# Causal attention between two spiking FFNs: another layout of the diagonal maximum units, scores first in a slot, and the loads of the next heads in two steps

## The reference

```python
scores = jnp.einsum('bhsd,bhtd->bhst', q, k) * scale
causal = jnp.triu(jnp.ones((S, S), dtype=bool), k=1)
scores = jnp.where(causal, -jnp.inf, scores)
probs = jax.nn.softmax(scores, axis=-1)
out = jnp.einsum('bhst,bhtd->bhsd', probs, v)
```

## Time and profile before

| | us |
|---|---|
| three runs | 1600.67, 1615.71, 1618.32 |
| median | 1615.71 |
| the profiled execution | 1608.4 |
| its span, first to last instruction | 1606.7 |
| PE busy | 1381.6 (86%) |
| DVE busy | 1139.5 (71%) |
| ACT busy | 860.6 (54%) |
| mean granted clock of PE | 0.904 of full speed |

### The profile page before, as it was taken

How to read it: one execution, slowest core, us unless ns; L and a number is a source line. 1 busy time by engine, 2 the same in 40 slices (tenths; PEclk the granted TensorE clock), 3 DMA queues, 4 the chain that set the end, 5 groups by cost and what they waited for, 6 DMA issues and landing times. The chain is left out here.

```text
span 1606.7 us, 27137 instructions
## 1 busy us (share of the span) xinstructions
PE 1381.6 (86%) x8384; PEld 821.8 (51%) x8384; DVE 1139.5 (71%) x2689; ACT 860.6 (54%) x1155; POOL 229.9 (14%) x206
## 2 busy tenths in 40 slices
PE   5988888750799999999999989999999976899997
PEld 5877777640443343343343333433433422799986
DVE  5666676821788888877887887888888930567675
ACT  5644444310036666655665665666666655466564
POOL 0012222346001011010010110110110101110100
PEclk9999999875568899997997999999999978899999
DMA  5113333437152062070080260440620002222312
GB/s 204 40 40 105 105 118 100 150 123 95 13 69 34 6 83 24 5 101 8 9 98 5 30 82 5 55 52 6 72 34 5 8 8 68 92 80 92 95 51 66
DMA packets 101898, 97.86 MB, mean 61 GB/s; under 512 B 46288, under 2 KB 85200, under 8 KB 100048
## 3 DMA queue, kind: packets, MB, share of 16 engines
q1 hardware_dynamic: 101744, 95.98, 29.0%
HBM read 57.15 MB, written 37.75 MB: 59 GB/s over the span
## 5 line engine op out<-in xcount | busy, mean ns | idle before, releaser
L1001 ACT ACTIVATE probs<-s_ps 128x1024 f32<-128x1024 f32 (+3 forms) x640 | 542.7, 895 | 327.7 <-PE s_ps L1133 326.4
L1112 PE MATMUL m_ps<-kT,qT 64*128 64x512 f32 (+3 forms) x1280 | 478.9, 478 | 112.9 <-DMA qT<-qkT_parts 55.9
L1026 DVE TENSOR_REDUCE maxes<-m_ps 128x1 f32<-128x512 f32 x768 | 490.8, 684 | 48.5 <-PE m_ps L1112 44.2
L1112 PEld LDWEIGHTS m_ps<-kT,qT 64*128 64x128 f32 x1280 | 217.2, 201 | 502.2 <-DVE maxes L1026 274.0
L1133 PE MATMUL s_ps<-qT,kT 64*128 64x512 f32 (+3 forms) x1280 | 327.3, 416 | 13.8 <-DMA qT<-shiftT 10.5
L1031 DVE CUSTOM_DVE_ANT_0 masked<-m_ps,mask_b 128x384 f32<-128x384 f32 (+3 forms) x512 | 238.3, 488 | 130.6 <-PE m_ps L1112 125.0
L1150 PE MATMUL o_ps<-probs,v_w 128*32 128x512 f32 (+3 forms) x2560 | 322.4, 578 | 0.2 <-POOL probs L974 0.2
L974 POOL TENSOR_SCALAR_AFFINE_SELECT probs<-probs 128x512 f32<-128x512 f32 x128 | 81.6, 637 | 851.8 <-ACT probs L1001 851.8
L1133 PEld LDWEIGHTS s_ps<-qT,kT 64*128 64x128 f32 x1280 | 164.2, 198 | 41.0 <-ACT probs L1001 25.0
L313 ACT ACTIVATE relu_a<-ups_a 128x512 f32<-128x512 f32 x64 | 38.1, 596 | 100.8 <-PE ups_a L562 99.9
L1150 PEld LDWEIGHTS o_ps<-probs,v_w 128*32 128x32 f32 x2560 | 51.9, 111 | 76.5 <-issue 58.9
(11 more groups left out here) (124 smaller groups left out, 1917.7 us busy)
## 6 DMA issues: line engine op xcount, KB each, us to landing
kT<-qkT_parts SPq DMA_DIRECT2D x48, 256.0 KB
qT<-qkT_parts SPq DMA_DIRECT2D x96, 128.0 KB
qkT_parts<-qk_hi_a SPq DMA_DIRECT2D x32, 256.0 KB, 3.0
qkT_parts<-qk_lo_a SPq DMA_DIRECT2D x32, 256.0 KB, 3.4
qT<-shiftT SPq DMA_DIRECT2D x512, 1.0 KB
xin_a<-in_x SPq DMA_DIRECT2D x8, 512.0 KB, 4.0
xres_a<-in_x SPq DMA_DIRECT2D x8, 512.0 KB, 4.9
x<-xsum_a SPq DMA_DIRECT2D x8, 512.0 KB, 3.2
```

What stands on the lines that cost most here:

```text
L1001: act.activation(probs[:, b % PBUF, 2 * hp:2 * hp + 2, off:CH], s_ps[hp][:, :, off:CH], ACT.Exp, scale=D ** -0.5)\
L1026: dve.tensor_reduce(out, m_ps[:, bank, 0:width], AX.X, ALU.max).then_inc(max_read, 1)
L1112: pe.matmul(m_ps[:, bank, 0:width], qT[of % 2][r0:r0 + HR, j, h // 2, t * P:(t + 1) * P], kT[of % 2][r0:r0 + HR, h // 2, k * CH:k * CH + w ...
```

## The change

Four edits, all in `attention_phase`. A diagonal square of a head and a step becomes three units in the place of four: TRI holds the four triangles of 128 keys side by side, over a mask that an identity matmul in bf16 writes into the bank first; WIDE and NARROW hold the rectangles between them, 512 and 256 columns. DVE reduces each with one `tensor_reduce` over several tiles. A group has 144 units. In a slot PE issues both head pairs' scores first and then the units. SP issues terms 0 and 1 of the next group's load at j = 0, and term 2 at j = 1. SP no longer waits for DVE before it loads the mask. The diff without empty lines:

```diff
-        mask = sb("mask_b", [P, CH])
-        masked = sb("masked", [P, 2, CH])
-        maxes = sb("maxes", [P, 2, G, T, NJ])
+        mask = sb("mask_b", [P, P])
+        masks, identb = sb("masks", [P, T, P], BF16), sb("identb", [P, P], BF16)
+        maxes = sb("maxes", [P, 2, G, T, FULL + NJ - 1])
...
-        UNITS = [(j, t, 2 * hp + par, k, CH if k < j else P * (t + 1))
-                 for j in range(NJ) for t in range(T) for hp in range(G // 2) for k in range(j + 1) for par in range(2)]
+        def diagonal(j, h):
+            k0 = j * CH
+            return [(j, h, [(t, t * P, k0 + t * P, P) for t in range(T)], CH, slice(0, T), TRI),
+                    (j, h, [(2, 0, k0, 2 * P), (3, 2 * P, k0, 2 * P)], CH, slice(2, 4), WIDE),
+                    (j, h, [(1, 0, k0, P), (3, P, k0 + 2 * P, P)], 2 * P, slice(1, 4, 2), NARROW)]
+        UNITS = []
+        for j in range(NJ):
+            UNITS += [(j, 2 * hp + par, [(t, 0, k * CH, CH)], CH, slice(t, t + 1), FULL + k)
+                      for t in range(T) for hp in range(G // 2) for k in range(j) for par in range(2)]
+            UNITS += [diagonal(j, 2 * hp + par)[part] for hp in range(G // 2) for part in range(3) for par in range(2)]
...
-            sp.wait_ge(mask_ok, 1)
-            sp.dma_start(mask[:, CH - P:CH], w["mask"]).then_inc(const_in, 16)
+            sp.dma_start(mask[:, :], w["mask"]).then_inc(const_in, 16)
...
-                if j < 3 and exists(i, dn + 1):
+                if j < 2 and exists(i, dn + 1):
...
-                    load(i, dn + 1, (j,))
+                    load(i, dn + 1, ((0, 1), (2,))[j])
...
-            dve.memset(mask[:, :], 0.0).then_inc(mask_ok, 1)
+            dve.memset(maxes[:, :, :, :, :], NEG).then_inc(neg_fill, 1)
             dve.wait_ge(const_in, 32)
+            dve.tensor_copy(masks[:, :, :], mask[:, :].unsqueeze(1).broadcast_to([P, T, P])).then_inc(mask_ok, 1)
+            dve.tensor_copy(identb[:, :], ident[:, :]).then_inc(mask_ok, 1)
...
-                out = maxes[:, j % 2, 2 * (h % 2) + h // 2, t, k:k + 1]
-                if k < j:
-                    dve.tensor_reduce(out, m_ps[:, bank, 0:width], AX.X, ALU.max).then_inc(max_read, 1)
-                else:
-                    dve.wait_ge(max_read, done - 1)
-                    dve.sem_inc(passed_max, 1)
-                    dve.tensor_tensor_reduce(masked[:, u % 2, 0:width], m_ps[:, bank, 0:width], mask[:, CH - width:CH], 1.0, NEG,
-                                             ALU.add, ALU.max, out).then_inc(max_read, 1)
+                out = maxes[:, j % 2, 2 * (h % 2) + h // 2, tiles, column]
+                dve.tensor_reduce(out, m_ps[:, bank, 0:width].rearrange("p (n c) -> p n c", n=out.shape[1]), AX.X, ALU.max)\
+                   .then_inc(max_read, 1)
...
+                if column == TRI:
+                    pe.matmul(m_ps[:, bank, :], identb[:, :], masks[:, :, :].rearrange("p t k -> p (t k)"), start=True, stop=True)
                 r0 = HR * (h % 2)
-                pe.matmul(m_ps[:, bank, 0:width], qT[of % 2][r0:r0 + HR, j, h // 2, t * P:(t + 1) * P],
-                          kT[of % 2][r0:r0 + HR, h // 2, k * CH:k * CH + width], start=True, stop=True)\
-                  .then_inc(max_done, 1)
+                for t, c0, k0, keys in pieces:
+                    mm = pe.matmul(m_ps[:, bank, c0:c0 + keys], qT[of % 2][r0:r0 + HR, j, h // 2, t * P:(t + 1) * P],
+                                   kT[of % 2][r0:r0 + HR, h // 2, k0:k0 + keys], start=(column != TRI), stop=True,
+                                   skip_group_check=True)
+                mm.then_inc(max_done, 1)
...
+                    scores(i, dn, j, b, 0)
+                    scores(i, dn, j, b, 1)
                     some(0)
-                    scores(i, dn, j, b, 0)
                     some(1)
-                    scores(i, dn, j, b, 1)
                     some(2)
...
-            pe.wait_ge(const_in, 32)
+            pe.wait_ge(mask_ok, 2)

```

More of the change, by code:

```diff
@@ L696, in attention_phase @@
         HR, MB = P // 2, 3
+        TRI, WIDE, NARROW, FULL = 0, 1, 2, 3
         qT = [sb(f"qT{p}", [P, NJ, G // 2, CH], F32R) for p in range(2)]
@@ L726, in attention_phase @@
         mask_ok, bias_in = sem("mask_ok"), sem("bias_in")
-        passed, passed_max = sem("passed_b"), sem("passed_max")
+        passed, neg_fill = sem("passed_b"), sem("neg_fill")
         o_read, denom_done, att_out = (sem(n) for n in ("o_read", "denom_done", "att_out"))
@@ L743, in attention_phase @@
         SLOTS = NJ * (NJ + 1) * T // 2
-        UNITS = [(j, t, 2 * hp + par, k, CH if k < j else P * (t + 1))
-                 for j in range(NJ) for t in range(T) for hp in range(G // 2) for k in range(j + 1) for par in range(2)]
+        def diagonal(j, h):
[8 more added lines that the diff above has]
+            UNITS += [diagonal(j, 2 * hp + par)[part] for hp in range(G // 2) for part in range(3) for par in range(2)]
         MAX_FROM, MAX_TO = -20, 20
         def place_units():
-            cost = [u[4] + 110 for u in UNITS]
+            cost = [u[3] + 110 for u in UNITS]
             room = []
@@ L1015, in _ @@
                 dve.memset(kT[0][HR * par + HR // 2:HR * (par + 1), :, :].bitcast(F32), 1.0).then_inc(ones_ok[0], 1)
-            dve.memset(mask[:, :], 0.0).then_inc(mask_ok, 1)
+            dve.memset(maxes[:, :, :, :, :], NEG).then_inc(neg_fill, 1)
             dve.wait_ge(const_in, 32)
+            dve.tensor_copy(masks[:, :, :], mask[:, :].unsqueeze(1).broadcast_to([P, T, P])).then_inc(mask_ok, 1)
+            dve.tensor_copy(identb[:, :], ident[:, :]).then_inc(mask_ok, 1)
+            dve.wait_ge(neg_fill, 1)
             def unit(i, dn, x, ahead, u):
-                j, t, h, k, width = UNITS[u]
+                j, h, _, width, tiles, column = UNITS[u]
                 done, bank, _ = ring(i, dn, x, (ahead, u))
                 dve.wait_ge(max_done, done + 1)
-                out = maxes[:, j % 2, 2 * (h % 2) + h // 2, t, k:k + 1]
-                if k < j:
-                    dve.tensor_reduce(out, m_ps[:, bank, 0:width], AX.X, ALU.max).then_inc(max_read, 1)
-                else:
-                    dve.wait_ge(max_read, done - 1)
-                    dve.sem_inc(passed_max, 1)
-                    dve.tensor_tensor_reduce(masked[:, u % 2, 0:width], m_ps[:, bank, 0:width], mask[:, CH - width:CH], 1.0, NEG,
-                                             ALU.add, ALU.max, out).then_inc(max_read, 1)
+                out = maxes[:, j % 2, 2 * (h % 2) + h // 2, tiles, column]
+                dve.tensor_reduce(out, m_ps[:, bank, 0:width].rearrange("p (n c) -> p n c", n=out.shape[1]), AX.X, ALU.max)\
+                   .then_inc(max_read, 1)
                 return done + 1
@@ L1040, in negate @@
                     dve.wait_ge(max_read, found)
-                    dve.tensor_reduce(negmax[:, :], maxes[:, j % 2, :, :, 0:j + 1].rearrange("p h t k -> p (h t) k"), AX.X,
+                    dve.tensor_reduce(negmax[:, :], maxes[:, j % 2, :, :, 0:FULL + j].rearrange("p h t k -> p (h t) k"), AX.X,
                                       ALU.max, negate=True).then_inc(neg_step, 1)
@@ L1105, in find @@
                 of = dn + ahead
-                j, t, h, k, width = UNITS[u]
+                j, h, pieces, _, _, column = UNITS[u]
                 if u == 0:
```

## The result

The changed kernel takes 1653.99 us (median of 4 runs, 1647.56 to 1656.59), beside 1611.97 for the kernel before on the same chip (4 runs, 1600.67 to 1618.32). The ratio is 1.0263, 95% interval 1.0193 to 1.0332: slower by 2.6%. The forecast was 1639. The two profiled executions have spans of 1654.2 and 1606.7 us, 47.5 apart.

The account below looks back on a forecast made before the run. It took a closed PE-DVE loop (2.71 us per four-unit slot) as the bound, with shifts and loads as separate limits. 1608.4 + 25 + 2.4 + 17.6 - 5.6 - 2 - 1.4 - 5 gave 1639; range 1602 to 1662.

Parts of the forecast that it names:

- slots 0 to 11, groups 1 to 6 (loads): Two-step load delays slot 12 through the shifts of j = 2: +5.0 in four groups, +2.4 in two, +25 us.
- slots 12 to 19: Masked units in slots 17 to 19, less savings from fewer units: +2.2 us a group, +17.6 in eight groups.
- slots 20 to 23: Four masked units hidden behind SP's shift queue: no added time, PE's 11.6 us staying under 13.9.
- slots 24 to 39, with the clock: Fewer units against masked units, -5.6 us in seven groups, and a third of the possible clock gain, -5.
- lead-in: Before the first exponential: 72 units for 87, less DVE work but eight masked units at low clock, -2 us.
- start: SP starts the first load without waiting for DVE's memset: -1.4 us.
- the new units' +1.2: Net cost in slots 0 to 11 a group, hidden by slot 12's wait in groups 1 to 6.
- The masked unit: A TRI holds PE 1.0 us: 0.35 to the first triangle, 0.13 between triangles; bounds 0.43 and 1.3.
- Scores first: Issuing both head pairs' scores first in a slot: loop unchanged, taken as 0; 0.1 us a slot without one reduce.
- Loads hidden: Rival: shifts overtake the load or DMA runs faster, so the +25 goes; centre 1616 us, chance 0.26.
- Faster, with triangles beside the other half's work: Rival: a TRI costs PE only 0.43 us and the loads are hidden; 1587 us, chance 0.14.
- Slower on PE with 1.3 us a masked unit: Rival: each triangle takes 0.23 us and PE's clock falls in TRI slots; 1667 us, chance 0.12.

Follow-up runs that it names:

- e2: The kernel before with only the two-step load added: 1655.35 us, ratio 1.0293.
- e1: The changed kernel with the old loads, one term at the start of each step: 1620.02 us, ratio 1.0091.
- e5: The changed kernel with two att tiles and load term 2 issued in slot 6, behind the shifts of j = 2: 1628.7 us, ratio 1.0166.
- e3: The changed kernel with two att tiles and a semaphore for each: 1652.93 us, ratio 1.0288.
- e7: The kernel of e1 without the identity matmul, so the maximum is computed unmasked: 1590.37 us, ratio 0.9906.
- e6: The changed kernel with the old loads and the old order in a slot, the new diagonal layout alone: 1621.18 us, ratio 1.0130.
- e4: The changed kernel with the old order in a slot, units between the two head pairs' scores: 1648.7 us, ratio 1.0243.
- e8: The kernel before with only the new order in a slot, both head pairs' scores first: 1616.14 us, ratio 1.0067.
- e10: The kernel of e1 with eight shift DMAs of two rows in place of sixteen of one: 1586.42 us, ratio 0.9859.
- e9: The kernel before with eight shift DMAs of two rows in place of sixteen of one: 1602.15 us, ratio 0.9995.
- e11: The kernel of e1 with the masked units of a head pair issued together: 1608.35 us, ratio 1.0008.
- e12: The kernel of e11 with eight shift DMAs of two rows: 1573.58 us, ratio 0.9782.

## Why the prediction was right in sign and too low

By its own steps, in us, from the two profiled executions:

| step | forecast | measured |
|---|---|---|
| slots 0 to 11, groups 1 to 6 (loads) | +25 | +42.0 |
| slots 0 to 11, groups 0 and 7 | +2.4 | +2.2 |
| slots 12 to 19 | +17.6 | +15.4 |
| slots 20 to 23 | 0 | 0.0 |
| slots 24 to 39, with the clock | -10.6 | -11.2 |
| lead-in | -2 | +2.0 |
| start | -1.4 | -2.1 |
| after the last exponential | 0 | -0.9 |
| sum, before rounding | +31.0 | +47.5 |

**The step that failed is the size of the loads' term**, +17.0 in a sum that is short by 16.5. Its mechanism was right: e2 shows it alone, e1 shows it gone, e5 shows that the queue's order is what matters. Two things in it were wrong.

First, groups 2 and 4. The prediction laid the new wait over the 2.62 us of the back edge and took 2.4 a group. They measure +7.4 and +4.7 (and +7 each in 4 to 11 in e2). The price had been worked out at slot 12 only. The store of slot 3 holds DVE already in slot 7, as the upper bound of the step had it, and from there the slots up to 11 are late; in group 2 the back edge comes after it and is paid again (2.04 us). In group 4 PE's stall there is 2.23 us and ends with the shifts. e3 shows the overlap that the prediction had reckoned with: without the store's wait the edge lies under the wait for the shifts, and the two groups measure +4.4 and +4.3. So some 3 us of group 2 are the store's, and the rest is what the second point says. The prediction had the store going out at 587 and landing at 596 to 598, and still priced slot 12 alone.

Second, the +5.0 in the other four groups measures +6.9 to +8.1. ACT begins slot 12 37.4 us after the load's begin, forecast 35.9. The load's packets are through early (about 604, forecast 606.1). The shifts' small packets run among the last of them, those of the store issued at 602.56 behind them; the DMA line above shows work until slice 36, that is 606 to 607 us, and PE's scores start at 608.03. The forecast end was 1.5 us too early for slot 12, though too late for the load's own data; what held the shifts' landing between 604 and 608 isn't shown. That what lies ahead of slot 12 is hidden by this end, as the prediction had it for the new units' +1.2, is borne out by e3.

**The masked unit** was forecast at 1.0 us of PE, 0.35 from the identity to the first triangle and 0.13 between triangles. Measured in slot 17 of group 1: 0.91 us; 0.32 to the first triangle, then steps of 0.164, 0.112 and 0.109, and 0.20 until the array can take the products. The forecast from the transposes gave 0.39 for three steps, the runs 0.385. The rule of the Trainium skill, "TensorE: Matmul & The Clock Gate", section "Packing small matmuls", lets a weight load overlap running matmuls only where the row group differs, which with the page's figure for a load was an estimate of 0.16 a step; the trace agrees for the first step and not for the other two.

**Slots 12 to 19** came to +15.4 for +17.6, and that it came so near is partly luck. Slots 17 to 19 were forecast at +2.9 a group and measure +1.6 (slot 17 +1.0 for +1.5, slots 18 and 19 +0.3 each for +0.7); e7 shows that the identity matmul is the whole of it. The -0.7 that was to come off isn't there: slot 13 is 0.5 to 0.8 shorter, but slot 14 is 0.4 to 0.7 longer (groups 1 and 3). The rest, +2.3, is in groups 1 and 4, where the clock in slots 12 to 16 was 0.88 and 0.83 for 1.00 and 0.91.

In **slots 0 to 3** the size was right (+2.3 to +2.5 a group from group 1 on, forecast +2.6) and the cause only in part. The identity matmul is 1.0 to 1.3 of it (e7, groups at the full clock). The order in a slot, which the prediction took as 0, is 1.5 of it: with the old order and the identity matmul the new units cost 0.9 to 1.0 a group there (e6, and e4 alike). The two shares overlap, so they aren't to be added. The old layout shows no such cost of the order (e8, slots 0 to 3 as before). **Slots 20 to 23** stayed at 14.0 to 14.3, behind SP's queue, as forecast. e10 shows what was under that cover: 10.7, where the prediction's terms had 11.6.

**The lead-in** has the wrong sign. Fifteen units fewer were to outweigh eight masked ones at the low clock. e7 gives the missing price: without the identity matmuls the lead-in is 6.2 us shorter, 0.8 for each of its eight units, where 0.35 at the high clock was the row to hand.

**Scores first** was taken as 0. In the changed kernel that holds for the sum (e4), though not for its parts: e1 against e6, in groups 1 to 6, has +1.5 us a group in slots 0 to 3, about +0.9 in 20 to 23 and in 28 to 30, -0.7 in 17 to 19 and -1.6 in 31 to 39. Alone it costs 0.7% (e8), most of it in slots 24 to 30, some of that at a lower clock. Why is open.

**Slots 24 to 39 and the clock.** That the -11.2 agrees with -10.6 is partly luck. It is made of -12.3 in slots 24 to 27, +17.8 in 28 to 30 (the TRIs, +2.5 a group as forecast) and -16.7 in 31 to 39. The -12.3 can't be put down to the units: before the change these slots take 13.4 to 15.6 us in the groups 0 to 3 with the clock at 0.77 to 0.87, and 11.7 to 12.1 in the groups 4 to 6 with the clock at 1.00; after it 11.5 to 12.9 at 0.68 to 0.87. Time at the lower clock fell only from 310 to 304 us of the program. **The start** can't be told from chance: among the kernels here that share the changed one's start it runs from -0.5 to -6.3 us, and two that have the start of the kernel before are at -3.1 (e2) and +1.1 (e9).

**The rivals.** Loads hidden: no, +42 us. Faster, with triangles beside the other half's work: not as the change has it. e11 issues them so, with its loads hidden, and is no faster than the kernel before (1.0008); e12 is 2.2% faster, most of it by the eight shifts. Slower on PE with 1.3 us a masked unit: 0.91.

## What to carry to other kernels

Count what stands in a DMA queue behind a load that is brought forward, small stores and small copies above all, and follow each to its reader; price the earliest reader and not only the one with the nearest deadline. A pause between bulk transfers can be what the small ones live on, so do not close it unless they go first. Where a wait covers an engine, look at what else stands behind the wait before you remove it, the granted clock above all: the same eight shifts gave nothing in the layout where the clock was low in that stretch in five of eight groups, and 2.3% in the one where it stayed at full speed.

## What the runs showed of the hardware

- A 128 KB store issued by the same queue right behind a load's terms took 9.8 us to land, where it took 5.0 behind one term and 1.9 alone.
- Sixteen shifts of 1 KB take SP 10.8 to 11.2 us to issue (12.1 once), eight shifts of 2 KB 4.3 to 4.5. The bytes are the same, so the cost goes with the number of DMAs, and the wider ones are a little cheaper each (0.54 for 0.67 us).
- Slots 20 to 23 of the old layout, with the eight shifts (e9), took 10.7 us at a granted clock of 1.00 and 14.3 at a mean of 0.64, between PE's two levels (2.4 and 1.2 GHz). PE was busy 8.8 us of those 10.7; in the new layout (e10) it was busy 10.2 of 10.7, and the clock there was 1.00 in all eight groups.
- Two full-height passes in a row, then half-height work on both halves in turn, cost PE less than two separate passages (0.93 us to the start of the last triangle for 1.62); in slots 20 to 23, once nothing else held them, e12 is 0.6 us a group shorter than e10.
- Four matmuls of 128 columns on one half of the rows started 0.164, 0.112 and 0.109 us apart behind a full-height pass.
- PE stood 2.6 us at the loop's back edge where the load's last term was issued behind it (e1), 5.4 (e5) and 7.0 to 8.1 (e9, e10, e12) where it was issued shortly ahead of it. The cause isn't isolated.
